# A four-layer network on one core: layer 4 turned into one stream of half sequences, and two-pass scores in layer 2

## The chip, the cores and the metric

The kernel runs on one core of a Trainium2 chip. The time is the device time of one execution in microseconds (us). Before the change it is 3823.37 us, the median of three runs (3819.16 to 3826.95).

## The reference, cut to what matters

Four sequences of 1024 tokens with 256 features go through four layers. Each computes `x = layernorm(x + f(x))`. The change touches the second and the fourth.

```python
# layer 2: 8 heads of 64, 8 experts; per head, causal
sim  = (q * 64**-0.5) @ k.T ;  attn = softmax(where(causal, sim, min))
out  = attn @ values        # values: from the expert that gates pick
out  = sum over heads of out @ output_experts[picked] * gate
# layer 4: per token, ternary weights, 256 -> 1024 -> 1024 -> 1024 -> 256
h = silu(x @ w1.T * s1) * (x @ w2.T * s2)
h = gelu(h @ h1.T * t1) ;  h = gelu(h @ h2.T * t2)
return h @ w3.T * s3
```

## The kernel before, in words

`program` calls `layer1` to `layer4`; each goes over the four sequences in a loop (`nc.Fori`) and leaves its sums, without the normalization, in DRAM. The next layer loads a sequence into `m.nx` and normalizes it there while it still works on the one before (`fetch_load`, `fetch_stats`, `fetch_sd`, `fetch_norm`, L120 to L153). Every engine has its own program, written by hand, and goes through it in order; they meet only in semaphores. An `nc.Block` ends with a barrier of all engines. There is no planner: the order of the calls in each engine's loop is the order on the chip.

**Split numbers.** A matmul on fp32 operands takes more passes than one on fp32r, which keeps fewer bits. So the kernel splits a value into hi (rounded to fp32r) and lo (the rest) and adds products of the parts. ACT rounds (`hi`), DVE or POOL subtracts (`lo`).

**Layer 2, `attention` (L590 to L786).** Heads go in pairs c; `project` (L629) makes keys and queries of two heads for half a sequence, four of them to a pair (`parts`), in fp32. `kst` holds key hi in one half of its 128 rows and key lo in the other, `qst` query hi in both, `qlo` query lo in both. In step `step`, head `step-1` has its maxima taken (`maxima`, L639: one fp32r pass over the causal half, then DVE's `reduce_max`, L769) and head `step-2` its scores, exps and weighted sum. A step has eight ticks k, one for each block of 128 keys: the largest block of queries comes first, 1024 columns at k = 0 and 128 at k = 7. `scores` (L653) makes for each of the 12 units of a head three passes and, on the diagonal, a short mask: keys by `qst`, keys by `qlo`, and the constant -1 by `shift`, which POOL builds at L785 as a diagonal matrix of the maxima. `weighted` (L668) is an fp32 product into PSUM bank 5 and 6 (`PV`). When a head's last `weighted` is done, DVE copies the result (`head_out`, L757) and ACT the row of denominators (`den_out`, L721); the next head's first `weighted` waits for both (L670 to L672). `hi_parts` (L706) and `lo_parts` (L742) are ACT's and DVE's share of a projection, and `project` waits for the `lo_parts` of the one before.

**Layer 4.** `fetch_first` (L156) normalizes the first sequence while the weights load, with barriers after it; one more block turns `misfit` into a flag. Then `net` (L1548) runs once a sequence: PE transposes eight tiles (`entry_transpose`, L197), ACT and DVE split them into `xhi` and `xlo`, and only then come the products of two half sequences n. A half is 16 products over `xhi`, `xlo` (4 passes each), 8 with `h1` and 8 with `h2` (16 passes each), and 4 output tiles with `w3` (16 passes of 256 columns). For each chunk ACT applies silu or gelu and rounds, and DVE multiplies (L1713) and subtracts (`split`, L1673). In the second half, after its second chunk, DVE runs `normed(0)` and `fetch_norm` (L1717 to L1719). PE picks its program with `pe.If(misfit > 0)`. After each sequence a block clears the semaphores.

Of the kernel before, what the change touches and what calls it, by code (L numbers as in the profile page):

```python
# [29 lines left out]
P = 128  # L30
D = 256
# [390 lines left out]
ATTN2 = ("qk_mm qk_hi qk_parts max_mm max_read shift_ready score_mm exp_ready pv_mm o_read den_read "  # L422
# [6 lines left out]
def layer2(nc, ctx, m, I, src, dst):  # L429
# [39 lines left out]

    def gates_and_values(own):  # L470
# [14 lines left out]
        with nc.Block() as block:  # L485
# [7 lines left out]
            def _(pe):  # L493
# [7 lines left out]
                for n, (h, t) in enumerate(order):  # L501
# [10 lines left out]
                    last.then_inc(s.value_mm, 1)  # L512

# [76 lines left out]
    def attention(own, b):  # L590
# [3 lines left out]
        kst, qst, qlo = (sb(n, [P, RK, T], F32R) for n in ("kst", "qst", "qlo"))  # L594
        shift = sb("shift", [P, 2, T], F32R)
        prob = sb("prob", [P, 2, T])
        mx = sb("mx", [P, H0, NT])
# [5 lines left out]
        parts = [(kind, n) for kind in "kq" for n in range(NH)]  # L603
        part_at = {0: 0, 1: 1, 2: 2, 4: 3}
# [10 lines left out]
        with nc.Block() as block:  # L615
            @block.sync
            def _(sp):
                fetch_load(sp, m, s, src[(b + 1) % SEQS])
                sp.dma_start(oe[:, :, :], I["oe2"][:, 0]).then_inc(s.oe_in, 16)
                for h in range(H0):  # L620
                    sp.wait_ge(s.den_read, h + 1)
                    sp.dma_start(dens[h:h + 1, :], den[den_row(h), h % 2, :]).then_inc((s.even_den_out, s.odd_den_out)[h % 2], 16)
                sp.wait_ge(s.even_den_out, 16 * (H0 // 2))
# [4 lines left out]
            def _(pe):  # L628
# [10 lines left out]
                def maxima(h, k):  # L639
                    t = NT - 1 - k  # L640
                    if k == 0:
                        pe.wait_ge(s.qk_parts, 4 * (h // 2 + 1))
# [10 lines left out]
                def scores(h, k):  # L653
                    for n, (kk, lo, hi) in enumerate(units, U * h):
                        if kk != k:
                            continue
                        if n % U == 0:
                            pe.wait_ge(s.shift_ready, NT * (h + 1))
                        if n >= 3:
                            pe.wait_ge(s.exp_ready, n - 2)  # L660
                        out, keys = bank(m.ps, n % 3, 0, hi - lo), kst[:, h % RK, k * P:(k + 1) * P]
                        pe.matmul(out, keys, qst[:, h % RK, lo:hi], start=True, stop=False)  # L662
# [15 lines left out]
                for step in range(H0 + 2):  # L678
                    h1, h2 = step - 1, step - 2
                    for k in range(NT):  # L680
                        if h2 >= 0:
                            scores(h2, k)
                        if step % 2 == 0 and step < H0 and k in part_at:
                            project(step // 2, part_at[k])
                        if 0 <= h1 < H0 and k < NT - 1:
                            maxima(h1, k)
# [1212 lines left out]
```

## Time and profile before

| | |
|---|---|
| median of three runs | 3823.37 us |
| the profiled execution: its time, its span | 3819.95 us, 3818.2 us |
| PE, DVE, ACT, POOL busy, share of the span | 88%, 55%, 38%, 22% |
| TensorE clock granted, mean | 0.930 of full |

A stretch of the profile shows for each engine how long it was busy. PE's matmuls are pipelined and overlap, so their cost is read from start to start. The views that the rows below come from read like this. Windows: the stretch, its length, then busy us (and instructions) of PE, of PE's weight loads, of DVE, ACT and POOL, then the granted clock, the DMA share and GB/s. Timeline: start, length, engine, line, operation, output and input, count; in brackets how long the engine stood idle before it and what released it. Lines: a group and its count, busy us, mean ns of one, idle us before them and what ended it. Waits: who waited for whom, us in total, times, the longest.

### The profile page before, as it was taken

Reading aid. Unit: us, or ns where it says so; the run is one execution under the profiler, and the core shown is the slowest. Engines: PE = TensorE matmul, PEld = TensorE weight load, DVE = VectorE, ACT = ScalarE, POOL = GpSimd, SP = SyncE. Lnnn points to the kernel's source line nnn. Section 1 sums busy time; section 2 is a strip of 40 time slices with the busy share of each in tenths; the row PEclk is TensorE's granted clock in tenths of the full one; section 3 lists DMA queues with packets and bytes.
Section 4 is the critical chain, followed back from the end, with each engine's and each line's share of the span. In section 5 each row is a group of like instructions: output and inputs, shape, how many; then the busy total and the mean of one; then the engine's idle time right before and its main releaser. Section 6 shows DMA issues by size and latency. Waiting matters only on the chain. (4 is left out here: it accounts for less than half of the span.)

```text
span 3818.2 us, 51310 instructions
## 1 busy us (share of the span) xinstructions
PE 3343.3 (88%) x18610; PEld 2417.7 (63%) x18610; DVE 2084.4 (55%) x3495; ACT 1465.2 (38%) x2638; POOL 830.3 (22%) x908
## 2 busy tenths in 40 slices
PE   6896898988989989888998698998989698989898
PEld 4555655975568755786558555546465476767676
DVE  4346844677445954569446474756657433333333
ACT  2321144412444134431344355563645433434343
POOL 1111411743137422454216300101010000000000
PEclk9897999988999999989999899998998899999999
DMA  5111100110011100111002101000000310000000
GB/s 180 44 44 56 44 1 24 52 40 28 1 45 42 35 22 1 68 32 44 1 1 75 56 2 24 1 13 13 2 23 2 117 52 12 12 12 12 12 12 12
DMA packets 139735, 121.01 MB, mean 32 GB/s; under 512 B 79696, under 2 KB 121936, under 8 KB 136016
## 3 DMA queue, kind: packets, MB, share of 16 engines
q1 hardware_dynamic: 139472, 117.45, 10.1%
q8 instruction: 172, 2.82, 0.3%
q14 instruction: 91, 0.75, 0.1%
HBM read 100.23 MB, written 28.31 MB: 34 GB/s over the span
## 5 line engine op out<-in xcount | busy, mean ns | idle before, releaser
L1378 ACT ACTIVATE l3b_prob<-sums 128x512 f32<-128x512 f32 (+3 forms) x768 | 333.0, 494 | 205.1 <-PE sums L1311 166.6
L1628 PE MATMUL sums<-l4a_uhi,l_h 128*128 128x512 f32 x1024 | 405.8, 396 | 0.0
L1628 PE MATMUL sums<-l4a_ulo,l_h 128*128 128x512 f32 x1024 | 403.8, 394 | 0.0
L842 POOL TENSOR_TENSOR l2c_rlo<-l2c_routed,l2c_rhi 128x512 fp32r<-128x512 f32 x256 | 348.4, 1374 | 214.0 <-ACT l2c_rhi L868 177.9
L769 DVE TENSOR_REDUCE l2b_mx<-sums 128x1 f32<-128x1024 f32 (+7 forms) x256 | 192.0, 757 | 318.9 <-PE sums L650 318.2
L703 ACT ACTIVATE l2b_prob<-sums 128x512 f32<-128x512 f32 (+3 forms) x384 | 186.6, 491 | 397.7 <-PE sums L666 393.2
L1673 DVE TENSOR_TENSOR l4a_ulo<-l4a_made,l4a_uhi 128x512 fp32r<-128x512 f32 x192 | 132.1, 688 | 375.1 <-ACT l4a_uhi L1641 374.2
L222 POOL COPY sb_x<-sb_nx 128x2048 f32<-128x2048 f32 x12 | 23.0, 1914 | 1322.6 <-POOLq L1742 571.1
L952 PE MATMUL sums<-l2c_ohi,l2c_rhi 128*128 128x256 f32 x1024 | 294.4, 287 | 12.8 <-POOL l2c_rlo L842 12.1
L674 PE MATMUL sums<-l2b_prob,l_vx 128*128 128x512 f32 (+3 forms) x768 | 301.0, 506 | 3.3 <-ACT l2b_den L725 1.9
L1306 PE MATMUL sums<-l_qst,l_kst 64*128 64x512 f32 (+3 forms) x768 | 279.3, 427 | 16.4 <-DMA l_qst<-l3b_peak 6.7
L952 PE MATMUL sums<-l2c_ohi,l2c_rlo 128*128 128x256 f32 x1024 | 291.9, 285 | 0.0
L952 PE MATMUL sums<-l2c_olo,l2c_rhi 128*128 128x256 f32 x1024 | 291.8, 285 | 0.0
L785 POOL TENSOR_SCALAR l2b_shift<-sb_ident,l2b_mx 128x128 fp32r<-128x128 f32 x256 | 154.2, 605 | 603.7 <-DVE l2b_mx L769 491.0
L1289 PE MATMUL sums<-l_kst,l_qst 64*128 64x512 f32 (+3 forms) x768 | 244.1, 443 | 18.9 <-DVE l3b_low L1390 10.4
L905 DVE TENSOR_TENSOR l2c_routed<-l_oT,sums 128x512 f32<-128x512 f32 x256 | 171.6, 682 | 149.3 <-PE sums L942 148.2
L868 ACT CAST l2c_rhi<-l2c_routed 128x512 fp32r<-128x512 f32 x256 | 158.2, 621 | 238.2 <-DVE l2c_routed L905 236.8
L1306 PEld LDWEIGHTS sums<-l_qst,l_kst 64*128 64x128 f32 x768 | 140.8, 195 | 153.9 <-ACT l3b_prob L1378 133.6
L203 PE MATMUL sums<-sb_ident,sb_nx 128*128 128x128 f32 x256 | 61.0, 421 | 194.4 <-issue 93.0
L1628 PEld LDWEIGHTS sums<-l4a_uhi,l_h 128*128 128x128 f32 x1024 | 192.4, 188 | 47.5
L1628 PEld LDWEIGHTS sums<-l4a_ulo,l_h 128*128 128x128 f32 x1024 | 192.4, 188 | 45.6
L662 PE MATMUL sums<-l2b_qst,l2b_kst 128*128 128x512 f32 (+3 forms) x384 | 207.5, 540 | 7.9 <-POOL l2b_shift L785 7.9
(247 smaller groups left out, 8141.3 us busy)
## 6 DMA issues: line engine op xcount, KB each, us to landing
l_ve<-ve SPq DMA_DIRECT2D x34, 512.0 KB, 4.0
l_oe<-oe SPq DMA_DIRECT2D x16, 1024.0 KB, 6.2
sb_nx<-sums SPq DMA_DIRECT2D x15, 1024.0 KB, 5.5
l2c_word<-weights_copy SPq DMA_DIRECT2D x32, 352.0 KB, 4.0
weights_copy<-h SPq DMA_DIRECT2D x2, 4096.0 KB, 25.9
l_qst<-l3b_peak SPq DMA_DIRECT2D x512, 0.5 KB, 2.0
l_h<-weights_copy SPq DMA_DIRECT2D x2, 4096.0 KB, 23.9
sb_nx<-tokens SPq DMA_DIRECT2D x5, 1024.0 KB, 5.7
```

Of the source, the lines that this page charges most:

```text
L662: pe.matmul(out, keys, qst[:, h % RK, lo:hi], start=True, stop=False)
L674: last = pe.matmul(bank(m.ps, PV, lo, hi), vx[:, k, h, :], prob[:, k % 2, lo:hi], start=(k == 0), stop=True, skip_group_check=True)
L703: act.activation(prob[:, k % 2, lo:hi], bank(m.ps, n % 3, 0, hi - lo), ACT.Exp, scale=SCALE0).then_inc(s.exp_ready, 1)
L769: dve.reduce_max(mx[:, h1, t:t + 1], bank(m.ps, max_bank(h1, k), 0, (t + 1) * P), AX_X).then_inc(s.max_read, 1)
L842: pool.tensor_tensor(rlo[:, i % RT, :], routed[:, i % RT, :], rhi[:, i % RT, :].bitcast(F32), ALU.subtract).then_inc(s.routed_lo, 1)
L868: act.copy(rhi[:, i % RT, :], routed[:, i % RT, :]).then_inc(s.routed_hi, 1)
L905: dve.tensor_tensor(routed[:, i % RT, :], oT[:, c, n * HALF:(n + 1) * HALF], bank(m.ps, 4 + i % 4), ALU.mult).then_inc(s.routed, 1)
L952: last = pe.matmul(m.ps[:, t * D:(t + 1) * D], r[:, k % RT, cols], w[:, c % 2, e, :], start=(c == e == 0 and t % 2 == 0 and r is rhi and w ...
L1289: last = pe.matmul(bank(m.ps, at, 0, hi - lo), qst[rows(a), p, t * P:(t + 1) * P], kst[rows(a), p, lo:hi], start=True, stop=True)
L1306: last = pe.matmul(bank(m.ps, part % SCORE, 0, hi - lo), kst[rows(a), p, k * P:(k + 1) * P], qst[rows(a), p, lo:hi], start=True, stop=True)
L1378: act.activation(prob[:, i % RB, j, a, 0:hi - lo], bank(m.ps, part % SCORE, 0, hi - lo), ACT.Exp, scale=SCALE1).then_inc(s.exp_ready, 1)
L1628: run(lambda out, a, x, first, last: pe.matmul(out, a, x, start=first, stop=last))
```

## The change

**Layer 2.** The pass `qlo` by `kst` and the pass with `shift` become one of 65 rows: 64 of key hi (`krow`) by query lo (`qrow`), and a 65th of -1 by the maximum. The product of the two lo parts is left out. ACT writes key hi a second time; DVE writes query lo once, not twice. The maxima come into row 65 by DMA, 128 values at a time, issued by SP; POOL's step is gone. The steps become a row of ticks x: head h's maxima at ticks 8 + 8h to 15 + 8h, its scores at 18 + 8h to 25 + 8h, projections of pair c in every other tick from 2 + 16c, in the order k0, k1, q1, q0. `head_out` and `den_out` come last in their tick, behind `hi_parts` and `lo_parts`. PE gets products that nobody reads (`warm`): eight at the end of the gates, eight after the first projections, one after each maximum of head 0.

```diff
-        parts = [(kind, n) for kind in "kq" for n in range(NH)]
-        part_at = {0: 0, 1: 1, 2: 2, 4: 3}
+        parts = [("k", 0), ("k", 1), ("q", 1), ("q", 0)]
+        WAIT = 2
+        APART = 2
...
+        scored_in = lambda x: divmod(x - 2 * NT - WAIT, NT)
+        peaked_in = lambda x: divmod(x - NT, NT)
```

SP, for each head h:

```diff
+                    for k in range(NT):
+                        t = NT - 1 - k
+                        sp.wait_ge(s.max_read, NT * h + k + 1)
+                        sp.dma_start(qrow[DH0:ROWS, h % RK, t * P:(t + 1) * P].bitcast(F32),
+                                     mx[:, h, t:t + 1].bitcast(F32)).then_inc(carried[h % 2], 16)
+                    if h >= 1:
+                        den_row_out(h - 1)
```

PE, `scores`, and below it the order of a tick:

```diff
-                            pe.wait_ge(s.shift_ready, NT * (h + 1))
+                            pe.wait_ge(s.qk_parts, 4 * (h // 2 + 1))
+                            pe.wait_ge(carried[h % 2], carried_to(h))
...
-                        pe.matmul(out, keys, qlo[:, h % RK, lo:hi], start=False, stop=False)
...
-                        pe.matmul(out, m.negones[:, :], shift[:, h % 2, lo:hi], start=False, stop=True).then_inc(s.score_mm, 1)
+                        pe.matmul(out, krow[0:ROWS, h % RK, at], qrow[0:ROWS, h % RK, lo:hi], start=False,
+                                  stop=True).then_inc(s.score_mm, 1)
...
+                    if has(h2):
+                        scores(h2, k2)
+                    if project_in(x):
+                        project(*project_in(x))
+                        if x == 3:
+                            warm(pe, 6, 8)
+                    if has(h1):
+                        maxima(h1, k1)
+                        if h1 == 0:
+                            warm(pe, PROJ, 1)
+                    h2, k2 = scored_in(x - 1)
+                    if has(h2):
+                        weighted(h2, k2)
```

DVE, the order of a tick (ACT's is exps, `hi_parts`, `den_out`):

```diff
+                    if has(h1):
+                        t = NT - 1 - k1
+                        dve.wait_ge(s.max_mm, NT * h1 + k1 + 1)
+                        dve.reduce_max(mx[:, h1, t:t + 1], bank(m.ps, max_bank(h1, k1), 0, (t + 1) * P), AX_X).then_inc(s.max_read, 1)
+                    if project_in(x):
+                        lo_parts(*project_in(x))
+                    if k2 == 0 and 1 <= h2 < H0:
+                        head_out(h2 - 1)
```

**Layer 4.** Loop, blocks and `fetch_first` go; one block holds eight half sequences (`UNITS`) written out. Each half is loaded, normalized and copied for itself (`next_stats`, `next_norm`, `residual`). The entry of half n + 1 (transposes, rounding, subtracting) stands between the `h2` products of half n. The lo parts of the first stage go from DVE to POOL. `normed(n - 1)` and `next_norm(n + 1)` stand in the `h1` stage. `scale` and `s3` are loaded behind `w2`, not behind all weights.

```diff
+                for n in range(UNITS):
...
+                            product(at(n, 0, o) + j, w, KC, o, lambda c: xhi[:, x, c, :], lambda c: xlo[:, x, c, :])
...
+                            if stage == 2 and 1 <= o <= OUTS and n + 1 < UNITS:
+                                entry(n + 1, o - 1)
```

DVE and POOL, for each half n:

```diff
+                for stage in (1, 2):
+                    for o in range(HC):
+                        split(n, stage, o)
+                        if stage == 1 and o == 0 and n:
+                            normed(n - 1)
+                        if stage == 1 and o == 2 and n + 1 < UNITS:
+                            next_norm(n + 1)
+                        if stage == 2 and 1 <= o <= OUTS and n + 1 < UNITS:
+                            next_lo(n + 1, o - 1)
+                outputs(n)
...
+                for o in range(HC):
+                    k = chunk(n, 0, o)
+                    pool.wait_ge(s.hi_ready, k + 1)
+                    pool.tensor_tensor(ulo[:, slot(n, 0), o, :], made[:, k % RT, :], uhi[:, slot(n, 0), o, :].bitcast(F32),
+                                       ALU.subtract).then_inc(s.h0_ready, 1)
```

## Rows read from the trace of the kernel before

**Rows 1.** The windows: layer 2, layer 4, layer 2's first attention.

```profile
318.00:2143.00 1825.00, 1612.27 (x8192) 1218.03 (x8192) 1117.00 (x1567) 606.19 (x1021) 713.11 (x800) 0.93 0.10 32
...
3032.00:3818.20 786.20, 685.51 (x3138) 560.37 (x3138) 282.50 (x635) 291.43 (x453) 7.58 (x4) 0.94 0.08 28
...
450.80:660.10 209.30, 188.57 (x768) 112.77 (x768) 97.77 (x149) 84.99 (x155) 38.54 (x64) 0.95 0.03 11
```

**Rows 2.** The timeline of PE across the end of a sequence in layer 4.

```profile
3423.44 0.28 PE L1628 MATMUL sums<-l_w,l4a_ulo 128*128 128x256 f32 x1
3437.07 3.68 PE L203 MATMUL sums<-sb_ident,sb_nx 128*128 128x128 f32 x16 [13.35 <-issue]
3443.86 0.47 PE L1628 MATMUL sums<-l4a_xhi,l_w 128*128 128x512 f32 x1 [3.11 <-issue]
```

**Rows 3.** The waits of layer 4 (us in total, times, longest).

```profile
PE sums L1628 <- issue: 16.5, 4, 6.7
...
PE sums L1628 <- DVE l4a_made L1713: 11.4, 4, 2.9
...
PE sums L1628 <- DVE l4a_ulo L1673: 4.1, 8, 0.5
```

**Rows 4.** The timeline of PE, full clock, in layer 4: 18 passes apart.

```profile
3269.41 0.39 PE L1628 MATMUL sums<-l4a_uhi,l_h 128*128 128x512 f32 x1
...
3273.61 0.39 PE L1628 MATMUL sums<-l4a_uhi,l_h 128*128 128x512 f32 x1
```

**Rows 5.** The timeline of layer 4's start: first load issued, first product.

```profile
3032.05 0.39 SPq L121 DMA_DIRECT2D sb_nx<-sums  x1
...
3057.67 0.76 PE L1628 MATMUL sums<-l4a_xhi,l_w 128*128 128x512 f32 x1 [6.66 <-issue]
```

**Rows 6.** The lines of POOL, by form: two subtractions of 512 columns.

```profile
L842 POOL TENSOR_TENSOR l2c_rlo<-l2c_routed,l2c_rhi 128x512 fp32r<-128x512 f32 x256 | 348.4, 1374 | 214.0 <-ACT l2c_rhi L868 177.9 <-PE sums L952 34.4
...
L1151 POOL TENSOR_TENSOR l3a_zlo<-l3a_z,l3a_zhi 128x512 fp32r<-128x512 f32 x32 | 52.3, 1644 | 107.3 <-ACT l3a_z L1117 107.3
```

**Rows 7.** The timeline of ACT: a first stage of layer 4 ends.

```profile
3270.40 0.63 ACT L1641 CAST l4a_uhi<-l4a_made 128x512 fp32r<-128x512 f32 x1 [0.52 <-DVE l4a_made L1713]
```

**Rows 8.** The lines of PE, by form: a 64-row pass, the pass removed.

```profile
L1306 PE MATMUL sums<-l_qst,l_kst 64*128 64x512 f32 x384 | 156.2, 478 | 11.5 <-DMA l_qst<-l3b_peak 6.7 <-ACT l3b_prob L1378 2.2
...
L663 PE MATMUL sums<-l2b_qlo,l2b_kst 128*128 128x512 f32 x192 | 78.8, 410 | 0.0
```

**Rows 9.** The timeline of PE in one attention: that pass and the next.

```profile
561.41 0.39 PE L663 MATMUL sums<-l2b_qlo,l2b_kst 128*128 128x512 f32 x1
561.64 0.39 PE L666 MATMUL sums<-l2b_shift,sb_negones 128*128 128x512 f32 x1
```

**Rows 10.** The timeline of DVE: results of heads 1, 2 and 3.

```profile
526.00 1.23 DVE L759 COPY l_oT<-sums 64x1024 f32<-64x1024 f32 x1 [0.98 <-PE sums L674]
...
554.56 1.22 DVE L759 COPY l_oT<-sums 64x1024 f32<-64x1024 f32 x1 [0.99 <-PE sums L674]
...
573.70 1.23 DVE L759 COPY l_oT<-sums 64x1024 f32<-64x1024 f32 x1 [0.98 <-PE sums L674]
```

**Rows 11.** The timeline of PE, ACT and DVE around one projection.

```profile
577.01 1.17 ACT L715 CAST l2b_kst<-sums 64x512 fp32r<-64x512 f32 x2 [0.24 <-PE sums L635]
...
578.81 1.39 DVE L749 TENSOR_TENSOR l2b_kst<-sums,l2b_kst 64x512 fp32r<-64x512 f32 x2
...
580.25 1.98 PE L635 MATMUL sums<-l_xT,l_wk 128*128 128x512 f32 x4 [1.34 <-DVE l2b_kst L749]
```

**Rows 12.** The timeline of PE: the first score of an attention.

```profile
474.94 0.80 PE L662 MATMUL sums<-l2b_qst,l2b_kst 128*128 128x512 f32 x1 [1.39 <-POOL l2b_shift L785]
```

**Rows 13.** The windows: four microseconds of layer 2's attention.

```profile
506.00:510.00 4.00, 4.00 (x15) 2.63 (x14) 1.14 (x2) 2.02 (x3) 0.00 (x0) 0.62 0.00 0
```

**Rows 14.** The lines of DVE by form: one maximum.

```profile
L769 DVE TENSOR_REDUCE l2b_mx<-sums 128x1 f32<-128x768 f32 x32 | 30.6, 957 | 68.3 <-PE sums L650 68.3
```

**Rows 15.** DMA issues by line: KB each, median us to landing.

```profile
l_qst<-l3b_peak SPq DMA_DIRECT2D x512, 0.5 KB, 2.0
```

More of the change, by code:

```diff
@@ L468, in layer2, with warm @@
     fetch_first(nc, m, s0, src[0], load, prepare)
+    def warm(pe, at, times):
+        for _ in range(times):
+            pe.matmul(bank(m.ps, at), sel[:, 0, :], sel[:, 0:HALF // P, :], start=True, stop=True)
     def gates_and_values(own):
@@ L602, in attention, with project_in @@
         through = lambda k: sum(kk <= k for kk, _lo, _hi in units)
-        parts = [(kind, n) for kind in "kq" for n in range(NH)]
-        part_at = {0: 0, 1: 1, 2: 2, 4: 3}
+        parts = [("k", 0), ("k", 1), ("q", 1), ("q", 0)]
+        WAIT = 2
+        APART = 2
+        ticks = NT * (H0 + 2) + WAIT + 1
+        scored_in = lambda x: divmod(x - 2 * NT - WAIT, NT)
+        peaked_in = lambda x: divmod(x - NT, NT)
+        has = lambda h: 0 <= h < H0
+        carried = (s.even_carried, s.odd_carried)
+        carried_to = lambda h: 16 * NT * (h // 2 + 1)
+        def project_in(x):
+            if x < 4:
+                return 0, x
+            c, ahead = divmod(x - WAIT, 2 * NT)
+            if 1 <= c < H0 // 2 and ahead in range(0, 4 * APART, APART):
+                return c, ahead // APART
         MAX, PV, PROJ = 3, 5, 7
@@ L676, in weighted @@
                     last.then_inc(s.pv_mm, 1)
[L678 to L686, printed above, removed]
-                        if h2 >= 0 and k >= 1:
-                            weighted(h2, k - 1)
-                        if 0 <= h1 < H0 and k == NT - 2:
-                            maxima(h1, NT - 1)
-                    if h2 >= 0:
-                        weighted(h2, NT - 1)
+                for x in range(ticks):
+                    h2, k2 = scored_in(x)
+                    h1, k1 = peaked_in(x)
+                    if has(h2):
[11 more added lines that the diff above has]
+                        weighted(h2, k2)
             @block.scalar
@@ L714, in hi_parts @@
                         if kind == "k":
-                            last = act.copy(kst[half(odd), slot, cols], got)
+                            act.copy(kst[half(odd), slot, cols], got)
+                            last = act.copy(krow[half(0), slot, cols], got)
                         else:
@@ L1533, in prepare, with at, chunk, slot @@
-    def prepare(dve):
-        dve.memset(ones[:, :], 1.0).then_inc(ld.ones, 1)
-    fetch_first(nc, m, s0, src[0], load, prepare)
-    with nc.Block() as block:
+    nx_in, y_out = (s.even_nx_in, s.odd_nx_in), (s.even_y_out, s.odd_y_out)
+    per_n = 4 * HC
+    def at(n, stage, o):
+        return per_n * n + (2 * o if stage == 0 else 2 * HC + (stage - 1) * HC + o)
+    def chunk(n, stage, o):
+        return HC * (3 * n + stage) + o
+    def slot(n, stage):
+        return (3 * n + stage) % 2
@@ new lines, in normed @@
+            def normed(n):
+                dve.wait_ge(s.y_sd, n + 1)
+                inverse_sd(y_step, dve, m, yr[:, n % 2, :], ymom[:, n % 2, :, 1], ysd[:, n % 2, :])
+                for j in range(OUTS):
+                    there = OUTS * (n % 2) + j
+                    dve.tensor_scalar(m.x[:, there, :], m.x[:, there, :], ymom[:, n % 2, j, 0:1], yr[:, n % 2, j:j + 1],
+                                      ALU.subtract, ALU.mult).then_inc(s.y_ready, 1)
+            dve.memset(ones[:, :], 1.0).then_inc(ld.ones, 1)
```

509 lines of the change are left out of this document (272 added, 237 removed).

## The prediction

> **What bounds the kernel now.** I read the page's first part, then the windows by layer, then inside layers 2 and 4 the timelines. PE is busy in 1612 of layer 2's 1825 us and 686 of layer 4's 786 [rows 1]; no other engine comes near, so in both layers the time is PE's products plus the gaps between them. In layer 4 the gaps are few and long: at the end of a sequence the last product starts at 3423.44 and the next sequence's first at 3443.86 [rows 2]. In layer 2's attention (209.3 us a sequence, [rows 1]) PE is nearly gapless, and what counts is how much it must do and whom it waits for. Layers 1 and 3 are untouched.
>
> **Layer 4, part by part.** Full-clock pitch of a 512-column pass: (3273.61 - 3269.41)/18 = 0.233 us [rows 4]; 256 columns take half, estimated. A half sequence is 320 passes and 64 short ones: 74.7 + 7.5 = 82.2 us, plus about 0.6 waiting for the last lo part before the output tiles (4.1 us over eight, [rows 3], and a longer first pass). Eight halves: 662.
>
> (1) The three boundaries go. Each costs 3443.86 - 3423.44 = 20.4 less one pass, 20.3 us [rows 2], of which transposes are 3.7; ten passes behind it run at half clock, +0.19 each, 2 us. Three times 22.3 = 67 us. (2) In each sequence PE waits 2.85 us for DVE's product, 11.4 in all [rows 3], because `normed` and `fetch_norm` stand in a stage where DVE is needed every 1.87 us; after it some eight passes run at 1.2 GHz, +1.5 us. In the new order these stand between `h1` splits, needed every 16 x 0.233 = 3.7 us and 0.69 long, with three buffers: 2.5 us fits. -17 us over four. (3) The start: first product 25.6 us after the first load is issued [rows 5]. Half as much to load and normalize saves some 4 us, two barriers and the flag's block some 3, the scales' earlier load one wait of 1.2 us, and the branch's 6.7 us "issue" [rows 5] stays, at most. I take -9; the ends are 0 and -14. (4) The tail loses a barrier, -1. (5) Added: 28 tiles are transposed inside the `h2` stage. At half clock 16 cost 3.7 us [rows 2], 0.23 each; at full clock half of that, and a switch between fp32 and fp32r of about 0.1: 28 x 0.37 = 10 us. Their ACT and DVE shares lie beside PE's 3.7 us per chunk. (6) POOL's lo part instead of DVE's: PE enters `h1` on 14 passes that need chunks 0 to 6, so chunk 7 may be 3.27 us late. Its rounding ends at 3270.40 + 0.63, 1.6 us behind the last product (3269.41). A subtraction on POOL takes 1.37 or 1.64 us in the two nearest places [rows 6, 7]: 3.0 to 3.3 us. I take 0; the ends are 0 and +3 us over eight halves. In steady state POOL needs 1.4 to 1.7 of 1.87 us, which holds.
> Sum for layer 4: -67 - 17 - 9 - 1 + 10 = -84 us, ends -70 and -92.
>
> **Layer 2, what goes.** The removed pass [rows 8] is 12 units a head: 6 of 512 columns, 2 each of 384, 256 and 128, at a pitch of 561.64 - 561.41 = 0.23 us [rows 9]; in the same timeline the shorter ones start 0.18, 0.12 and 0.12 apart. That is 2.25 us a head, 18 a sequence, 72 in all. The 65-row pass replaces one of 128 rows. Nearest row: 64 rows, 478 ns against 410 in the removed pass, though the first has waits and PSUM bank changes in it [rows 8]; bounds 0 and +0.07 x 384 = +27 us; I take 0, since its neighbours of equal columns start equally far apart.
>
> **Layer 2, what comes in its place.** Full-clock ticks, from pitches: odd heads 15.2 us of passes and some 0.1 us for each change between fp32r and fp32, 16.1; with four projections of 1.71 us, 23.2. Before, they take 573.70 - 554.56 = 19.1 (odd) and 554.56 - 526.00 = 28.6 (even) [rows 10], that is 18.35 and 25.5 of work and 0.8 and 3.1 of waits. Now follow an even head (2 or 4) in the new order, P = end of its first projection. ACT now writes a key part four times 64 x 512, not twice: 2 x 1.17 [rows 11], so P + 2.5. DVE's lo part, 1.39 [rows 11]: P + 4.1. Only then, in the same tick, comes `head_out`, 1.23 [rows 10]: P + 5.4. PE has in between the last `weighted` of the old head and one tick of scores and maxima: it stands at `weighted(h, 0)` from P + 2.1 and waits 3.4 us for `o_read`. Behind it on PE's queue stand the next scores, so ACT and DVE starve after it too. In odd heads, head 6 and head 7 no projection is in the way, but DVE's maximum (0.96, [rows 14]) is: `head_out` ends 2.2 us behind the last product, PE comes 1.3 behind it: 0.9 us (0.7 in head 7). Further: the query parts are projected two short ticks apart (3.0 us of PE work against a chain of 4.1), 1.2 us in each of three even heads; at the seventh and eighth tick a maximum waits for the one before, 0.6; and in the eighth tick of an even head a maximum is behind a lo part, 1.1.
> Adding these, from first score to the end of a sequence: head 0 24.9, heads 1, 3, 5 18.6 each, heads 2 and 4 28.3 each, head 6 (no maxima in its last two ticks) 16.0, head 7 14.0: 167.3 us. Before: from 474.94 [rows 12] to 656.9, where the last result is copied, 182.0. So -14.7 of 18: five sixths of the pass is gained where nothing is projected, and next to nothing in heads 2 and 4.
> The clock: after a wait of about 1.3 us between many short ones, PE ran at 0.62 in 506:510 [rows 13], half clock for some 3 us, 1.5 us lost, and the first scores run at half clock too. The new waits of 3.4 us (two a sequence) may do the same. I charge 2 us a sequence; ends 0 and 3.4.
> Start of an attention: ACT writes 16 pieces of 0.585 ahead of DVE's last lo part; the first maximum starts about 2 us sooner, two maxima of head 1 now stand ahead of the first score, and the `warm` products lie in waits. -0.5 us; ends +1 and -3. The rows carried by DMA: landing takes 2.0 us [rows 15]; from a head's last maximum to its first score lie some 3.9 us of PE work. Cost 0, with 1.9 us of cover; without it the wait shows directly at each head. POOL's 605 ns steps and DVE's second lo copy had cover and bring nothing. SP also issues the denominators between two heads' rows; it is one or two rows late then and has six ticks to catch up.
> Sum for layer 2: 4 x (-14.7 + 2 - 0.5) = -53 us; ends -20 (every wait doubled by a slow clock, half of the 65-row bound) and -80 (no new waits).
> A rule that speaks against this: the Trainium skill (TensorE: Matmul & The Clock Gate, What's actually happening) says that the slow clock is the default and activity releases it. By it both long waits a sequence would be followed by a slow stretch: 8 x 1.7 = 14 us, of which my 2 us a sequence already hold 8.
>
> **The sum.** -84 - 53 = -137 us on 3819.95, the profiled execution's own time (span 3818.2): 3683. The median of the runs is 3.4 above it: 3686 us.
>
> **Rivals.** (a) The copy of a finished head behind the lo parts eats the pass: each of the two waits brings a slow stretch, the odd heads lose their 0.9 twice, and layer 2 brings 20 us. For it: DVE is in order and two projections share the tick with `head_out`. Against: [rows 10] show 3.1 us of waits in even heads already. 3823 - 84 - 20 = 3719. (b) The waits don't come, because ACT and DVE run ahead where I let them wait: layer 2 brings 80, 3823 - 84 - 80 = 3659. (c) Layer 4's stream isn't gapless: the straight program of eight halves waits for instructions as it does now behind the branch (3.3 us at four places, [rows 3]), once in each stage of each half: 32 x 1.7 = 54 us lost, 3740. Against: in the loops nothing of the kind shows inside a half of 700 instructions. (d) Slower than before: the rows carried by DMA are late. Each of 32 heads then starts its scores late by what the landing exceeds 3.9 us. It cancels the rest from 137/32 = 4.3 us of wait, a landing of 8.2 us, four times [rows 15]; at 9 us it gives 3686 + 32 x 5.1 = 3849. For it: a 1 MB load and the experts' 1 MB are on the same queue, but only at the start of an attention. (e) The change doesn't do what it says in layer 4, the entry being late for its half: a load is issued a whole half (82 us) ahead, so no.
>
> **How the numbers follow.** Forecast 0.58; (a) 0.17; (b) 0.13; (c) 0.07; (d) 0.02; the rest (e, or an unseen cost that leaves it within 0.2% or above) 0.03. Its own range is 3668 to 3708; for 8 in 10 the range reaches to (b) and to (a): 3658 to 3725. A change of 0.2% (7.6 us) is about what the measurement can tell: faster 0.96, within it 0.01, slower 0.03.
>
> **What would show it.** In layer 4: no pause of PE over 1 us from the first product to the last, 28 transposed tiles between `h2` products at full clock, a stretch of about 675 us. If the pauses sit at the entry of `h1`, POOL is late. In layer 2: three product lines less one, head results copied 28, 18.5, 28, 18.5 us apart, PE's longest waits at the fp32 product of `weighted` for DVE's copy into `l_oT`, and none for the DMA row. If even heads take 25 us or less, (b) was right; over 30, (a). An attention of more than 205 us, or a layer 4 of more than 720, would make the prediction wrong.

## The result, and the profile after

The changed kernel takes 3691.65 us (median of four runs, 3685.81 to 3697.23) against 3821.26 us, 0.9655 of the time before (95% interval 0.9632 to 0.9678): 130 us less between the medians, where 137 were forecast (3686 us, range 3658 to 3725). The profiled execution took 3697.23 us, its span 3695.5. The forecast is near; of its two parts one is right to 3 us and the other 14 us too high.

The windows of the changed kernel, one for layers 1, 2, 3 and 4 each, cut at the first load that a layer issues (columns: stretch, length, then busy us and instructions of PE, weight loads, DVE, ACT and POOL, granted clock, DMA share, GB/s):

```profile
0.00:317.40 317.40, 261.91 (x864) 162.26 (x864) 130.69 (x378) 87.48 (x158) 49.73 (x68) 0.94 0.25 84
317.40:2104.00 1786.60, 1556.12 (x7904) 1158.40 (x7904) 1071.21 (x1503) 635.39 (x1085) 571.66 (x548) 0.94 0.11 33
2104.00:2995.90 891.90, 786.49 (x6416) 480.54 (x6416) 554.11 (x915) 480.98 (x1006) 59.82 (x36) 0.92 0.09 16
2995.90:3695.50 699.60, 670.18 (x3138) 548.28 (x3138) 241.08 (x562) 290.43 (x457) 90.63 (x72) 0.98 0.08 29
```

Against [rows 1], layer 4 went from 786.2 to 699.6 us, -86.6 (forecast -84), and layer 2 from 1825 to 1786.6, -38.5 (forecast -53). Layers 1 and 3, whose code is the same, moved by -0.6 and +3.

**Layer 4.** The waits of the changed kernel there (us in total, times, longest; the rows of PE):

```profile
PE sums L1584 <- DVE l_ones L1771: 8.1, 1, 8.1
PE sums L1659 <- issue: 7.4, 1, 7.4
PE sums L1595 <- DVE sb_nx L1732: 7.1, 1, 7.1
PE sums L1659 <- DVE l_ulo L1745: 4.1, 8, 0.5
PE sums L1595 <- DVE l_xlo L1738: 0.5, 1, 0.5
```

All but the fourth stand ahead of the first product (3013.55, that is 17.6 us behind the first load, where [rows 5] have 25.6). From there on PE stops for nothing but the last low part ahead of the output tiles, as in [rows 3]; the waits for `made`, 11.4 us in [rows 3], and the pauses between sequences [rows 2] are gone. What the entry costs inside the third stage can be read from DVE's low parts, one for each chunk of PE's work (timeline of DVE; start, length, wait before):

```profile
3233.00 0.69 DVE L1745 TENSOR_TENSOR l_ulo<-l_made,l_uhi 128x512 fp32r<-128x512 f32 x1 [3.04 <-ACT l_uhi L1676]
3236.73 0.69 DVE L1745 TENSOR_TENSOR l_ulo<-l_made,l_uhi 128x512 fp32r<-128x512 f32 x1 [3.04 <-ACT l_uhi L1676]
3237.34 0.42 DVE L1738 TENSOR_TENSOR l_xlo<-sums,l_xhi 128x256 fp32r<-128x256 f32 x1
3240.69 0.69 DVE L1745 TENSOR_TENSOR l_ulo<-l_made,l_uhi 128x512 fp32r<-128x512 f32 x1 [2.93 <-ACT l_uhi L1676]
```

A chunk without a tile takes 3.73 us, one with a tile 3.96: 0.23 us a tile, 6.4 for 28. The stores of one half follow those of the last after 83.87 us (3122.49, 3206.35, 3290.22, and so on).

**Layer 2.** An attention, from the issue of its first load to that of the next block's, takes 199.8, 196.8, 198.8 and 200.1 us, where before it took 209.3, 210.1, 207.6 and 209.8: 41 us less over four. PE's waits in the first one:

```profile
PE sums L685 <- DVE l2b_mx L806: 9.4, 12, 3.2
PE sums L713 <- DVE l_oT L798: 5.9, 2, 3.0
PE sums L713 <- ACT l2b_prob L743: 3.1, 5, 0.8
PE sums L669 <- PEq L489: 2.8, 1, 2.8
PE sums L669 <- DVE l2b_qrow L792: 2.0, 3, 0.7
PE sums L713 <- ACT l2b_den L766: 0.6, 1, 0.6
```

The second row is the wait that the prediction placed at `weighted(h, 0)`. Its second case in the timeline of ACT, DVE and PE:

```profile
570.37 0.58 ACT L756 CAST l2b_krow<-sums 64x512 fp32r<-64x512 f32 x1
570.98 1.00 ACT L766 COPY l2b_den<-sums 1x1024 f32<-1x1024 f32 x1
570.99 1.39 DVE L789 TENSOR_TENSOR l2b_kst<-sums,l2b_kst 64x512 fp32r<-64x512 f32 x2 [0.90 <-ACT l2b_krow L756]
572.41 1.23 DVE L798 COPY l_oT<-sums 64x1024 f32<-64x1024 f32 x1
...
573.74 3.75 PE L713 MATMUL sums<-l2b_prob,l_vx 128*128 128x512 f32 x4 [2.97 <-DVE l_oT L798]
```

Head 3's last product had ended at 569.4. ACT rounds a key part four times before `den_out` (570.98) gets its turn, DVE subtracts before `head_out` (572.41) does; PE waits 2.97 us. Its next four fp32 passes take 3.75 us, where the same four took 1.94 at 480.71: half clock. In the windows:

```profile
551.00:573.00 22.00, 18.86 (x83) 10.90 (x82) 8.82 (x12) 9.83 (x20) 0.00 (x0) 1.00 0.03 0
573.00:583.00 10.00, 9.27 (x22) 4.56 (x22) 2.15 (x3) 2.73 (x6) 0.00 (x0) 0.66 0.04 2
583.00:600.00 17.00, 15.14 (x66) 8.56 (x65) 8.42 (x12) 9.26 (x18) 0.00 (x0) 1.00 0.02 0
```

### The profile page after: what moved, and what is told of

Read it like the earlier page. It is cut to its first block and busy times, and to the rows that moved or that the text cites. A ratio compares the mean times of both kernels' runs of the same rounds, so it can differ in the third digit from the quotient of the medians.

```text
span 3695.5 us, 50581 instructions
## 1 busy us (share of the span) xinstructions
PE 3274.7 (89%) x18322; PEld 2349.5 (64%) x18322; DVE 1997.1 (54%) x3358; ACT 1494.3 (40%) x2706; POOL 771.8 (21%) x724
## 5 line engine op out<-in xcount | busy, mean ns | idle before, releaser
L1659 PE MATMUL sums<-l_uhi,l_h 128*128 128x512 f32 x1024 | 405.8, 396 | 0.0
L1659 PE MATMUL sums<-l_ulo,l_h 128*128 128x512 f32 x1024 | 405.6, 396 | 0.0
L806 DVE TENSOR_REDUCE l2b_mx<-sums 128x1 fp32r<-128x1024 f32 (+7 forms) x256 | 193.0, 757 | 315.7 <-PE sums L687 313.8
L1745 DVE TENSOR_TENSOR l_ulo<-l_made,l_uhi 128x512 fp32r<-128x512 f32 x128 | 90.5, 707 | 362.2 <-ACT l_uhi L1676 362.1
L1659 PEld LDWEIGHTS sums<-l_ulo,l_h 128*128 128x128 f32 x1024 | 192.3, 188 | 46.1
L1659 PEld LDWEIGHTS sums<-l_uhi,l_h 128*128 128x128 f32 x1024 | 192.2, 188 | 45.1
L514 PE MATMUL sums<-l2a_vhi,l2a_xhi 128*128 128x512 f32 x512 | 204.3, 399 | 15.8 <-DVE l2a_vm L564 12.2
L701 PE MATMUL sums<-l2b_qst,l2b_kst 128*128 128x512 f32 (+3 forms) x384 | 218.0, 568 | 0.0
L984 PEld LDWEIGHTS sums<-l2c_ohi,l2c_rhi 128*128 128x128 f32 x1024 | 198.4, 194 | 21.9 <-issue 21.9
L984 PEld LDWEIGHTS sums<-l2c_olo,l2c_rhi 128*128 128x128 f32 x1024 | 197.9, 193 | 10.2
## 6 DMA issues: line engine op xcount, KB each, us to landing
weights_copy<-h SPq DMA_DIRECT2D x2, 4096.0 KB, 25.7
```

The lines of the kernel that those rows point to most:

```text
L514: last = pe.matmul(bank(m.ps, n % RING), x[:, c, t * P:(t + 1) * P], v[:, h % 2, c, :], start=(c == 0 and x is xhi and v is vhi), stop=(c ...
L701: pe.matmul(out, kst[:, h % RK, at], qst[:, h % RK, lo:hi], start=True, stop=False)
L806: dve.reduce_max(mx[:, h1, t:t + 1], bank(m.ps, max_bank(h1, k1), 0, (t + 1) * P), AX_X).then_inc(s.max_read, 1)
L984: last = pe.matmul(m.ps[:, t * D:(t + 1) * D], r[:, k % RT, cols], w[:, c % 2, e, :], start=(c == e == 0 and t % 2 == 0 and r is rhi and w ...
L1659: run(lambda out, a, x, first, last: pe.matmul(out, a, x, start=first, stop=last))
```

## Experiments

Each is compared with the kernel before on its own chip; the changed kernel, run so a second time (`e10_changed_again`), gave 3688.57 us, 0.9666 (0.9648 to 0.9683). "Four attentions" is the sum of the four, from the trace: 836.8 us before, 795.5 and 795.3 in two profiles of the changed kernel. How far such sums can be read is seen where the code is the same: the seven profiles with the changed layer 2 as it is have 791.1 to 797.2 us, and layer 3, which no experiment touches, takes 882.2 to 898.4 us in all fourteen. So a few us between two profiles say nothing, and a layer's own time says more than the kernel's. The diffs are cut to the lines that matter, and some are abridged.

**Each layer's part by itself.**

```diff
 # e2_layer2_only: layer2 as changed, layer4 as before
 # e3_layer4_only: layer2 as before, layer4 as changed
```

> The kernel before with only layer 2 changed (layer 4 as before). Theory (the two parts are independent, layer 2's share is what its loads showed, 38.6 us): 3821 - 39 = 3782, ratio 0.990; layer 4 takes 786 us. Rival (the prediction's -53 was right and the one profile read it short): 3768, ratio 0.986.

> The kernel before with only layer 4 changed (layer 2 as before). Theory: 3821 - 87 = 3734, ratio 0.977; layer 4 takes 699 to 700 us, attention 207 to 210. Rival (part of layer 4's gain needs the shorter layer 2, or part of it shows up elsewhere): a ratio over 0.981.

Measured: 3784.72 us, 0.9902 (0.987 to 0.9933), and 3742.33 us, 0.979 (0.9764 to 0.9816), 39 and 81 us less. Together that is 120 of 130, which the intervals (10 to 12 us either way) can't tell from the whole. Four attentions take 795.2 and 838.8 us, so layer 2's share is the same with either layer 4. The first experiment's rival, 0.986, lies just outside the interval, and the traces speak against it too: its attentions take 198.8 us on average, those of the changed kernel 198.9. Layer 4 took 705.0 us in the second and not 699.6: its stores follow at 83.86 us as in the changed kernel, and the 5 us lie in the first half.

**The copies of a finished head first.**

```diff
 # ACT, in each tick
+                    if k2 == 0 and 1 <= h2 < H0:
+                        den_out(h2 - 1)
                     if project_in(x):
                         hi_parts(*project_in(x))
-                    if k2 == 0 and 1 <= h2 < H0:
-                        den_out(h2 - 1)
 # DVE: head_out(h2 - 1) ahead of lo_parts(...) in the same way
```

> The changed kernel, in whose attention the copies of a finished head (head_out on DVE, den_out on ACT) stand ahead of the parts of a projection in the same tick instead of behind them. Theory (the copy queued behind the lo part makes PE wait 2.97 us twice a sequence, and five of these eight waits are followed by a granted clock of 0.62 to 0.86 over some 9 us): the waits of PE for l_oT fall from 6 us to under 1 us a sequence, 24 us in all; the slow stretches behind them give back up to 11 us more; the lo parts come 1.2 us later and have two ticks of cover. An attention goes from 198.9 us to 190 to 193, the kernel to 3656 to 3671, ratio to the kernel before 0.957 to 0.961. Rival (PE is held next by something as late, the rounding or the lo part it now waits for at its next projection): the l_oT wait goes but attention stays at 197 to 200, kernel 3685 to 3697.

Measured: 3655.99 us, 0.9573 (0.9547 to 0.96), 33 to 36 us under the changed kernel. Four attentions take 765.0 us, 30.5 less. The wait in its timeline:

```profile
522.93 1.23 DVE L798 COPY l_oT<-sums 64x1024 f32<-64x1024 f32 x1
...
524.26 1.95 PE L713 MATMUL sums<-l2b_prob,l_vx 128*128 128x512 f32 x4 [0.68 <-issue]
```

The copy of head 1 starts 73.4 us behind the attention's first load, where it was 75.6; PE waits 0.7 us at this place, and its other waits stay at 9.4, 3.1 and 2.0 us, so nothing takes the old wait's place. In a sequence 5.9 us of waits became 1.4: 18 of the 30.5 us over four. Of the other 12, 10 lie in the stretches of heads 2 and 4, from copy to copy: each is 24.9 us now, and 24.8 to 27.8 in the changed kernel, where the clock was slow in five of eight. The last 2 lie ahead of head 0's copy and are within the spread. So the order of a few lines cost a quarter of what the whole change brought.

**What a pass is worth.**

```diff
 # e4_pass_twice: the new order with three passes again
+                        pe.matmul(out, kst[...], qst[...], start=True, stop=True)
                         pe.matmul(out, kst[...], qst[...], start=True, stop=False)
 # e5_old_less_pass: the order before, with two
-                        pe.matmul(out, keys, qlo[:, h % RK, lo:hi], start=False, stop=False)
```

> The changed kernel with the first of its two score passes made twice (the second overwrites the first; no number changes), so as many passes as before the change in the new order. Theory 1 (PE sets the pace in nearly all of attention, so a pass is worth its 2.25 us a head, 18 us a sequence, and the new order gave some 8 us of it back in its own waits): an attention goes from 198.9 to 213 to 217 us, four of them to +56 to +72 us, kernel 3748 to 3764, ratio 0.981 to 0.985. Theory 2 (a pass is worth only what the change showed, 10.3 us a sequence, the rest of it lying beside other engines' work): +41 us, an attention of 209, kernel 3733, ratio 0.977.

> The kernel before with only the products of the queries' low part left out of the scores (so their low bits are missing from the result); order, maxima, POOL's diagonal and DVE's second low copy as before. It prices the pass in the old order, beside the 9.4 us a sequence that a second pass added to the new one. Theory 1 (odd heads and head 6 of the old order are full of products, 18.99 of 19.1 us and 18.80 of 18.80, even heads are held in part by other engines): 2 us off each of heads 1, 3, 5, 6, 7 and 1 off heads 0, 2, 4, 12 to 13 us a sequence, attention 196 to 198, kernel 3821 - 50 = 3771, ratio 0.987; then the new order as a whole brought nothing beside the pass. Theory 2 (a pass is worth 9.4 us in either order): attention 200, kernel 3783, ratio 0.990.

Measured: 3741.28 us, 0.9791 (0.9767 to 0.9814), and 3788.94 us, 0.9909 (0.9881 to 0.9937). With the change they make a square:

```text
four attentions, us    three passes   two passes    the pass
order before              836.8          806.8        30.0
order after               833.5          795.5        38.0
new order brings            3.3           11.3
```

Theory 1 falls in both: the removed pass, 2.25 us a head back to back and 72 us over 32 heads, is worth 30 to 38, half of it. Theory 2 is near in both: attentions of 208.4 us where it had 209, and of 201.7 where it had 200. (The kernel's medians have 50 us between two passes and three in the new order; 6.5 of them are layer 3's in the two profiles.) The 8 us between 30 and 38, or between 3.3 and 11.3, are little more than the spread of equal code, and the clock had a part in them, as shown below. Where it counts is seen in the copies of the finished heads (timeline of DVE). In the order before, less the pass:

```profile
505.30 1.22 DVE L758 COPY l_oT<-sums 64x1024 f32<-64x1024 f32 x1 [0.86 <-PE sums L673]
523.75 1.23 DVE L758 COPY l_oT<-sums 64x1024 f32<-64x1024 f32 x1 [0.87 <-PE sums L673]
553.42 1.22 DVE L758 COPY l_oT<-sums 64x1024 f32<-64x1024 f32 x1 [0.87 <-PE sums L673]
572.15 1.23 DVE L758 COPY l_oT<-sums 64x1024 f32<-64x1024 f32 x1 [0.87 <-PE sums L673]
600.13 1.22 DVE L758 COPY l_oT<-sums 64x1024 f32<-64x1024 f32 x1 [0.87 <-PE sums L673]
617.61 1.23 DVE L758 COPY l_oT<-sums 64x1024 f32<-64x1024 f32 x1 [0.87 <-PE sums L673]
```

Head 0 ends 54.2 to 55.2 us behind an attention's first load, with the pass 54.2 to 55.3, and heads 2 and 4 take 29.7 and 28.0 us against 28.6 of [rows 10]; head 5, an odd one, takes 17.5 against 19.1. In the new order the same: with the pass made twice head 0 ends 53.7 us behind the attention's first load, with it once 53.9; heads 1 and 3 take 1.7 us more with it, heads 5, 6 and 7 1.7, 1.8 and 0.9, and heads 2 and 4, at full clock, 25.7 against 24.8. So a pass counts for most in the heads in which nothing is projected, and for 0.9 of its 2.25 us in those with a projection. That ACT's roundings, DVE's low parts and the maxima set the pace there is read from the waits, not shown by a run. In the order before, a part went to the clock too: the windows 505:524, 524:551 and 551:569 were granted 0.91, 0.94 and 0.91 without the pass, and 0.91, 1.00 and 1.00 with it, some 3 us in this sequence. A wait that the pass had covered then comes out: those for `l2b_prob` are 3.1 us with the pass made once and 0.7 with it made twice (new order, first attention), those for a maximum 9.4 and 6.0.

**The start of an attention.**

```diff
 # on top of the copies first; only for the first pair
-                            last = act.copy(krow[...], got)   # behind each kst copy
+                    if x == 2:                                # behind the first query part
+                        keep(0)                               # both krow copies of k part 0
+                        keep(1)
 # DVE
+                    if project_in(x) and x != 3:
                         lo_parts(*project_in(x))
+                    if x == NT + 3:
+                        lo_parts(0, 3)
```

> The kernel of the experiment with the copies first, in which at the start of an attention ACT writes the second copy of head 0's and 1's key parts (krow) behind the first query part's copies instead of ahead of them, and DVE makes the low part of the last query part four ticks later, behind the fourth maximum of head 0. Theory (up to the first score the bound is the chain of ACT's copies and then DVE's maxima: 8 key copies of 0.58 us stand ahead of the first maximum, then DVE is idle 1.0 us for a rounding): the first maximum comes 1.2 us sooner, the first reduction 3 us sooner, the first score 2 to 3 us sooner, 0 to 1 us given back since more of the first products run at half clock: attention 191.3 - 2.5 = 188 to 189.5, kernel 3656 - 10 = 3643 to 3650. Rival (PE's own products at half clock set the start): first score less than 1 us sooner, kernel 3652 to 3657.

Measured: 3651.77 us, 0.9564 (0.9549 to 0.9578), the fastest of all, though not told from the copies first by the intervals. Its four attentions take 759.2 us, 5.8 less, where 7 to 13 were expected, and as much as equal code can differ. PE's first row of `scores` starts 21.4 us behind the first load and not 24.1, but there the products run at half clock (timeline of PE):

```profile
471.34 0.78 PE L702 MATMUL sums<-l2b_qst,l2b_kst 128*128 128x512 f32 x1
...
473.43 3.60 PE L669 MATMUL sums<-l_xT,l_wk 128*128 128x512 f32 x4
```

The projection takes 3.60 us; with the copies first alone, begun at 475.69, it took 2.42. Over the four sequences the first scores come 10.5 us sooner, and the stretch from there to the copy of head 0 is 4.7 us longer: the mechanism is the one expected, and nearly half of the gain goes straight back to the clock.

**Without the products that only keep PE busy.**

```diff
-        for _ in range(times):
+        for _ in range(0):
             pe.matmul(bank(m.ps, at), sel[:, 0, :], sel[:, 0:HALF // P, :], start=True, stop=True)
```

> The changed kernel without the added products that only keep PE busy in layer 2 (eight behind the gates, eight behind the first projections, one behind each maximum of head 0). Theory: the start of an attention is held by ACT's and DVE's chain (first maximum 460.8, first score 474.3), so the granted clock of 450:474 falls from 0.85 to 0.7 and the time by nothing to 2 us a sequence: 0 to +8 us. Rival (the clock there decides): first score 4 us later and more scores at half clock, +20 us, ratio 0.971.

Measured: 3704.16 us, 0.969 (0.9655 to 0.9725), between the two, though its interval meets that of the changed kernel. Four attentions take 805.6 us, 10 more, which is beyond the spread. The granted clock of the first 24 us is 0.72, as expected, where the changed kernel has 0.86:

```profile
451.00:475.00 24.00, 16.35 (x40) 8.12 (x41) 12.47 (x17) 9.09 (x16) 3.50 (x1) 0.72 0.28 88
475.00:479.00 4.00, 4.00 (x10) 2.25 (x10) 1.09 (x1) 1.19 (x2) 0.00 (x0) 0.55 0.04 0
```

Head 0 ends 0.4 us later in the first attention and 2.8 later in the third, 5 over all four; the other 5 are that more of the waits for `l_oT` are followed by half clock: heads 2 and 4 take 26.4 to 27.8 us in all four attentions, where 24.8 is full speed. I can't say why.

**Layer 4's entry behind the half, and its normalizing in the first stage.**

```diff
 # e6_entry_behind
-                            if stage == 2 and 1 <= o <= OUTS and n + 1 < UNITS:
-                                entry(n + 1, o - 1)
+                    if n + 1 < UNITS:               # behind the output tiles
+                        for j in range(OUTS):
+                            entry(n + 1, j)
 # e7_norm_in_first: DVE (ACT's roots at o == 1, the next input's statistics at o == 0)
+                    if o == 2:                      # first stage
+                        normed(n - 1); next_norm(n + 1)
-                        if stage == 1 and o == 0 and n:
-                            normed(n - 1)
-                        if stage == 1 and o == 2 and n + 1 < UNITS:
-                            next_norm(n + 1)
 # e11, e12: the first stage's low parts on DVE, in the changed kernel and in e7
-                    pool.tensor_tensor(ulo[...], made[...], uhi[...], ALU.subtract)
+                    if o: first_split(n, o - 1)     # DVE, behind the chunk's product
```

> The changed kernel, in whose layer 4 the next half's four tiles are transposed behind the output tiles of this half, and not between the products of its third stage; the rest of the stream (no barriers, halves, early loads) stays. Theory (a boundary of before was 20.3 us, of which the entry's own chain of transposes, hi and lo is the smaller part): at each of seven boundaries PE waits for the output's copies out of its two banks, then for the last tile's hi and lo parts, 5 us, then some products run at half clock, 2 us, and 0.9 us of transposes leave the stage: +6 us each, +42 in all, layer 4 742 us, ratio 0.976 to 0.978. Rival (the gain came from interleaving the entry, the barriers cost little): +15 to +20 us each, 0.995.

> The changed kernel, in whose layer 4 the normalizing of the last half's output and of the next half's input (2.3 and 2.4 us of DVE, with ACT's square roots) stand in the first stage again, at its third chunk, where DVE is needed every 1.87 us, and not between two splits of the second stage. Theory: before, 6.05 us of this kind made PE wait 2.85, so 3.2 us are covered; 4.7 us leave 1.5 us uncovered, less what POOL's taking of the low parts freed on DVE, and POOL must catch up: 0 to 2 us in each of seven halves, 0 to +14 us, layer 4 700 to 714. Rival (each is worth the 4.3 us a time that the prediction gave for the move): +30 us, layer 4 730.

> The changed kernel with the low parts of layer 4's first stage made by DVE again, behind the next chunk's product, and not by POOL. Theory (DVE then needs 0.75 + 0.69 = 1.44 of each 1.87 us and keeps up; POOL's place was worth nothing in this order): no wait of PE inside a half, layer 4 699 to 702 us, kernel 3685 to 3697, ratio 0.965 to 0.968. Rival (DVE falls behind at the stage's statistics of the next input and PE waits for its product): 1 to 3 us in each half, +8 to +24 us.

> The kernel of the experiment with the normalizing in the first stage, with that stage's low parts on DVE instead of POOL. There, beside POOL's subtractions, DVE's four-element steps with two SBUF inputs took 842 and 1088 ns on average where they take 162 and 222 in the changed kernel, and PE waited 3.1 us a half. Theory 1 (POOL's and DVE's operations get in each other's way, and the stretched steps are what makes the wait long): with POOL idle these steps take 162 and 222 ns again, DVE is away 4.7 us as against 6.05 us before, and PE waits 1.5 us a half: layer 4 from 738.6 to 712 to 726 us, ratio 0.970 to 0.974. Theory 2 (DVE's being away for 4.7 us is what costs): the steps shrink, but DVE now also has the low parts to do, and layer 4 stays at 735 to 745 us, ratio 0.977.

Measured, with layer 4 from the traces:

```text
                        us       ratio (95%)                layer 4
before                                                      786.2
changed              3691.65   0.9655 (0.9632 to 0.9678)    699.6
entry behind         3730.0    0.9758 (0.9728 to 0.9788)    731.8
norm in first        3732.13   0.9771 (0.9743 to 0.9798)    738.6
low on DVE           3690.83   0.9658 (0.9636 to 0.9679)    698.8
norm first, low DVE  3715.62   0.9727 (0.9706 to 0.9748)    725.0
```

With the entry behind the half, layer 4 still gains 54 of 87 us: so much is everything else together, the barriers dropped, the normalizing moved and the shorter start. 32 are the interleaving, 4.6 us at each of seven boundaries; 6 were expected, and the rival's 15 to 20 fall. POOL's place is worth nothing, as forecast.

My theory on the normalizing was wrong and its rival too low: 39 us, 4.9 a half. PE waits 24.8 us for DVE's product, eight times, 3.7 at most. DVE's steps on four elements, by line and form (count, busy us, mean ns), in that kernel:

```profile
L115 DVE SCALAR_TENSOR_TENSOR l_ysd<-l_ymom,sb_eps,l_ysd 128x4 f32<-128x4 f32 x8 | 8.7, 1088 | 0.3
L114 DVE TENSOR_TENSOR l_ysd<-l_yr 128x4 f32<-128x4 f32 x8 | 6.7, 842 | 0.3
```

and with the low parts on DVE, where the wait is 15.5 us, six times:

```profile
L115 DVE SCALAR_TENSOR_TENSOR l_ysd<-l_ymom,sb_eps,l_ysd 128x4 f32<-128x4 f32 x8 | 1.8, 223 | 0.3
...
L114 DVE TENSOR_TENSOR l_ysd<-l_yr 128x4 f32<-128x4 f32 x8 | 1.3, 164 | 0.3
```

One case, with POOL's low parts on (timeline of the kernel with the normalizing in the first stage):

```profile
3104.13 2.55 POOL L1817 TENSOR_TENSOR l_ulo<-l_made,l_uhi 128x512 fp32r<-128x512 f32 x2 [3.02 <-ACT l_uhi L1676]
...
3104.30 0.17 DVE L113 RECIPROCAL l_yr<-l_ysd 128x4 f32<-128x4 f32 x1
...
3104.51 0.94 DVE L114 TENSOR_TENSOR l_ysd<-l_yr 128x4 f32<-128x4 f32 x1
...
3105.49 1.22 DVE L115 SCALAR_TENSOR_TENSOR l_ysd<-l_ymom,sb_eps,l_ysd 128x4 f32<-128x4 f32 x1
...
3106.74 0.17 DVE L116 TENSOR_SCALAR l_ysd<-l_ysd 128x4 f32<-128x4 f32 x1
```

The first row is two subtractions back to back, the first up to 3105.43, the second from 3105.39 to 3106.68. `L114` starts beside the first and ends with it, at 3105.45; `L115` starts beside the second and ends with it, at 3106.71. `L113`, with one tensor input, stands beside the first subtraction too and takes 0.17 us as ever. `L116` and what follows run behind both and are no evidence either way. Each of the two steps stands on four elements a partition and takes 0.16 and 0.22 us where POOL is idle. So DVE was away 6.5 us (from 3104.30 to its next product at 3110.79) and not the 4.7 that I had added up from rows in which POOL was idle. Theory 1 of the last experiment holds, at its upper end: taking POOL out gives 13.6 us back although DVE has more to do. The other 25 us are DVE's absence itself: 15.5 us of waits, and 8 us of slow clock, which five of the six waits have behind them, 1.5 to 1.7 us each.

## Why the prediction was nearly right, and the step that failed

**Layer 4: right.** Start: forecast -9, measured -8.0. Transposes: +10 forecast, +6.4 measured; 0.23 us a tile and not 0.37, the switch costs less than I took. POOL's low parts: 0, as taken. The stall in mid-sequence: -17 forecast, 4.3 us each; the trace of before has 13. PE's waits of 11.4 us are gone, but only the first of the four had a slow clock behind it, 1.7 us (windows of before, the first two of four stalls; the other two have 1.00 as well):

```profile
3157.50:3167.50 10.00, 9.98 (x36) 7.99 (x37) 7.73 (x12) 7.33 (x11) 0.00 (x0) 0.83 0.01 2
3350.70:3360.70 10.00, 9.96 (x43) 8.06 (x44) 7.59 (x12) 8.59 (x13) 0.00 (x0) 1.00 0.01 2
```

The forecast had charged one to each. The boundaries: -67 forecast; the three pauses of before are 20.7, 20.4 and 20.4 us from the last product to the first, less a pass each, and the 10 us behind them lack 2.1, 1.7 and 2.2 us of clock, together 67. The tail, last product to end, is 10.4 us and was 12.8: -2.4 where -1 was forecast. Added up, -8 - 67 - 13 - 2.4 + 6.4 is -84, and 2.6 of the 86.6 us are left over. So the forecast's -84 hit the time by its biggest term and by luck in the small ones: the stall taken 4 us too high, the transposes 3.6 too dear. Rivals (c) and (e) are refuted: from the first product on PE waits nowhere more than 0.5 us.

**Layer 2: right in kind, 14 us short.** The wait for `o_read` came at the place named, in two heads of each sequence, 3.0 us and not 3.4. The slow clock behind it cost more than I charged. Around the eight waits the granted clocks are 1.00, 0.62, 1.00, 0.86, 1.00, 0.69, 0.81 and 0.83 over 9 to 12 us, which lack 12 us of full clock; 10 to 12 came back with the copies first. I had charged 8. The rule of the Trainium skill (TensorE: Matmul & The Clock Gate, What's actually happening), that the slow clock is the default and activity releases it, was weighed ahead at 14 us. That was nearer in the sum, though three of the eight waits had no slow stretch behind them. The rows carried by DMA never made PE wait, as taken, and the 65-row pass costs what the 128-row one in its place did: 440 ns, against 441 of the pass with `shift`.

The head results come otherwise than the prediction's signs had them. It had 28 and 18.5 us for an even and an odd head, and said that even heads of 25 us or less would show rival (b), no new waits. Even heads take 24.8 us at full clock, as head 2 does here (timeline of DVE, the copies of heads 1, 2 and 3):

```profile
525.87 1.23 DVE L798 COPY l_oT<-sums 64x1024 f32<-64x1024 f32 x1
...
550.67 1.21 DVE L798 COPY l_oT<-sums 64x1024 f32<-64x1024 f32 x1
...
572.41 1.23 DVE L798 COPY l_oT<-sums 64x1024 f32<-64x1024 f32 x1
```

Still the waits are there. What is late is the copy of the odd head itself, so the wait lies in the odd head's stretch from copy to copy, 21.7 us, and the two together are 46.5, where 46.9 were forecast. The sum was right, and the sign pointed at the wrong head.

**The step that failed** is the sum "head 0 24.9": from the first score (474.27) to the copy of head 0 (504.14) it was 29.9 us, 5.0 more. The seven others together, from that copy to the last, took 142.7 us against 142.4, but with 3 us of slow clock that I had charged elsewhere. I had taken head 0 for an even head without the wait, and such a head does take 24.9 (copies first, 522.93 to 547.82). What I left out is that `weighted` runs a tick behind the scores, so that the first head's stretch has nine ticks: counted from its own first score, head 2 takes 29.5 us with the copies first and not 24.9. And its first products run at half clock (0.58 in 474.3:478), though I had named it. The one sequence of that kernel in which they don't, the fourth, has 28.4 us: 3.5 of the 5.0 us are the ninth tick, 1.5 the clock. Before the change the stretch was 30.4 (474.94 to 505.30): the pass brought 0.5 there, and "five sixths of the pass is gained" was too much: the two experiments on the pass put it at half. From the first score to the last copy the first sequence took 172.6 us against 169.3 with its 2 us of clock, 3.3 more. The four attentions together gave 41.3 us where 53 were forecast, so 12 of layer 2's 14 us are missing in them, and 3 lie outside of them, as much as equal code can differ.

**The rivals.** (a) was nearer than its chance of 0.17 said: layer 2 brought 39, about half way between its 20 and the forecast's 53, and its mechanism, the copy behind the low parts, is the one that cost 30 us. But the pass wasn't eaten by it alone. (b) is refuted by the waits, (d) by the absence of any wait for a DMA row. (In five other profiles one or two waits of 1.3 us ahead of a first score are put down to such a DMA. They stand at a product for a maximum, which doesn't read the row, and here the same wait of 1.3 us is put down to DVE's maximum.)

## What to carry to other kernels

Price a removed pass by stage: take from the trace how full the engine is in each kind of head (or tile), and count the pass only where it is full; here 72 us of products were worth 30 to 38. When you place a wait, say also in whose stretch it will show: a late copy lengthens its own head, not the next. On each in-order engine put what frees a buffer ahead of what only prepares the next round: two moved calls gave 33 to 36 us. And take a duration from rows in which the engines that share a path are as busy as they will be.

## What the runs showed of the hardware

Two of DVE's operations with two tensor inputs in SBUF stretched five- to sixfold beside POOL's subtraction (162 to 944 ns, 222 to 1216 ns, in seven cases of eight), and one with a single input (`L113`, 0.17 us) didn't. The Trainium skill (SBUF — State Buffer, Who interferes with whom) says that a DVE instruction with two SBUF inputs contends with a GpSimd instruction that reads SBUF, and one with at most one SBUF input, outside certain modes, does not. The traces agree, and show how long it lasts here: both steps ended within 0.03 us of the end of the subtraction beside them (1290 ns each), that is, they waited it out.

After a wait of 2.6 to 3 us PE's granted clock falls to half for several us in some cases and not in others, with the same program at the same place: behind the second wait of the first sequence the window 573:582 had 0.62 in one profile and 0.81 in the next, behind the first wait of the second sequence 964:973 had 1.00 and 0.62. Before the change one of four waits of 2.85 us in layer 4 was followed by it; with the normalizing in the first stage and the low parts on DVE, five of six waits of 2.6 us. Which waits are followed by it stays open.
